# A written-out order of work for five engines, drawn up anew ahead of and behind a loop

## What is computed

```python
B, S, H = 4, 1024, 384          # NUM_HEADS = 6, HEAD_SIZE = 64, NEG = -9e15
h = jnp.maximum(_layernorm(x, axis=-1), 0.0)
q, k, v = (_heads(h @ W + b) for W, b in ((Wq, bq), (Wk, bk), (Wv, bv)))
scores = jnp.einsum('bhqd,bhkd->bhqk', q, k) / np.sqrt(HEAD_SIZE)
probs = jax.nn.softmax(scores + jnp.where(graph_mask, 0.0, NEG)[:, None], axis=-1)
ctx = jnp.einsum('bhqk,bhkd->bhqd', probs, v)
return x + ctx @ Wf + bf          # x is (64, 128, 384), adj is (64, 128, 128)
```

## Time and profile before

| what | value |
|---|---|
| time, median of 3 runs | 475.81 us (474.95 to 476.01) |
| span of the profiled execution, first to last instruction | 473.5 us |
| median time less that span | 2.3 us |
| TensorE busy | 461.8 us |
| VectorE, ScalarE, GpSimd busy | 369.9, 366.1, 303.6 us |
| granted TensorE clock, as the record has it | 1.00 in all 40 slices |
| one group in the loop | 28.0 us |

### The profile page before, as it was taken

One profiled execution on the slowest core, in us unless ns is written; L12 is line 12 of the kernel. 1 busy time (PEld: TensorE's weight loads), 2 busy tenths in 40 slices (PEclk: granted clock), 3 DMA queues, 4 the chain that ended last, 5 costly groups with the idle time before them and its releaser, 6 DMA issues.

```text
span 473.5 us, 12912 instructions
## 1 busy us (share of the span) xinstructions
PE 461.8 (98%) x4457; PEld 273.0 (58%) x4457; DVE 369.9 (78%) x746; ACT 366.1 (77%) x820; POOL 303.6 (64%) x307
## 2 busy tenths in 40 slices
PE   7989999999999999999999999999999999999996
PEld 3645556556465565746556475665646556464763
DVE  5988979868888696886869688695987788687954
ACT  4879898876887887877788787788878877876950
POOL 3376767777678565767756576765667577533852
PEclk9999999999999999999999999999999999999999
DMA  8153959989979797896959679694969979776995
GB/s 302 61 118 90 162 112 169 187 182 215 187 138 225 118 194 175 184 199 124 215 123 213 155 156 214 130 213 80 217 147 164 239 120 163 184 108 150 150 192 162
DMA packets 219615, 78.56 MB, mean 166 GB/s; under 512 B 199472, under 2 KB 219568, under 8 KB 219568
## 3 DMA queue, kind: packets, MB, share of 16 engines
q1 hardware_dynamic: 209200, 65.63, 71.0%
q10 hardware_dynamic: 10368, 12.33, 9.6%
HBM read 16.19 MB, written 12.58 MB: 61 GB/s over the span
## 4 chain that ended last, share of the span: by engine, by line
PE 80%; DVE 6%; SPq 5%; issue 2%; POOL 2%; DMA 2%; ACT 2%; ACTq 0%; POOLq 0%; DVEq 0%
PE ps_proj L995 23%; PE ps_proj L997 22%; PE ps_proj L996 22%; PE ps_scores L1060 7%; SPq L565 2%; PE ps_ctx L995 2%; SPq L557 2%; PE ps_ctx L996 2%; PE ps_ctx L997 2%; PE ps_proj L1123 1%; DMA ht_parts<-h_pairs 1%; DMA ct_parts<-ctx_parts 1%; DVE shift_by L820 1%; POOL probs_parts L637 1%; DVE stats L807 1%
## 5 line engine op out<-in xcount | busy, mean ns | idle before, releaser
L637 POOL TENSOR_TENSOR probs_parts<-probs,probs_parts 128x768 f16<-128x768 f32 x64 | 105.3, 1646 | 35.2 <-ACT probs_parts L751 35.0
L736 ACT ACTIVATE probs<-masked,neg_max 128x128 f32<-128x128 f32 x384 | 118.5, 389 | 8.0 <-DVE neg_max L867 6.7
L995 PE MATMUL ps_proj<-ht_parts,w_hi 128*128 128x512 f16 (+1 forms) x309 | 109.8, 361 | 1.7 <-DVE qkt_lo L839 0.8
L996 PE MATMUL ps_proj<-ht_parts,w_hi 128*128 128x512 f16 (+1 forms) x309 | 109.7, 360 | 0.0
L997 PE MATMUL ps_proj<-ht_parts,w_lo 128*128 128x512 f16 (+1 forms) x309 | 109.7, 360 | 0.0
L720 ACT ACTIVATE qkt_hi<-ps_proj,bias_qk 128x512 f16<-128x512 f32 x94 | 63.6, 680 | 40.5 <-PE ps_proj L997 39.9
L643 POOL TENSOR_TENSOR ctx_parts<-ctx_sb,ctx_parts 128x384 f16<-128x384 f32 x62 | 56.9, 918 | 52.1 <-ACT ctx_parts L757 51.9
L839 DVE SCALAR_TENSOR_TENSOR qkt_lo<-ps_proj,bias_qk,qkt_hi 128x512 f16<-128x512 f32 x94 | 68.7, 740 | 22.0 <-ACT qkt_hi L720 22.0
L858 DVE SCALAR_TENSOR_TENSOR masked<-ps_scores,score_unscale,mask 128x384 f32<-128x384 f32 x128 | 72.5, 609 | 8.4 <-PE ps_scores L1060 8.4
L622 POOL TENSOR_TENSOR h_pairs<-h_sb,h_pairs 128x384 f16<-128x384 f32 x60 | 54.5, 917 | 37.6 <-ACT h_sb L711 37.5
L632 POOL TENSOR_TENSOR x_bf<-x_sb,b_out 128x384 f32<-128x384 f32 x64 | 63.1, 999 | 5.2 <-DVE y_sb L890 3.9
(11 more groups left out here) (102 smaller groups left out, 918.5 us busy)
## 6 DMA issues: line engine op xcount, KB each, us to landing
y<-y_sb SPq DMA_DIRECT2D x64, 192.0 KB, 2.6
x_sb<-in_x ACTq DMA_DIRECT2D x56, 192.0 KB, 3.2
x_sb<-in_x SPq DMA_DIRECT2D x8, 192.0 KB, 5.6
pt_parts<-probs_parts SPq DMA_TRANSPOSE x64, 4.0
ct_parts<-ctx_parts SPq DMA_TRANSPOSE x62, 3.0
adj_sb<-in_adj ACTq DMA_DIRECT2D x14, 64.0 KB, 2.8
w_raw<-in_Wk SPq DMA_DIRECT2D x1, 576.0 KB, 6.2
w_raw<-in_Wv SPq DMA_DIRECT2D x1, 576.0 KB, 7.3
```

What stands on the lines that cost most here:

```text
L637: nc.gpsimd.tensor_tensor(probs_parts[b][:, 1, :], probs[b % 2][:], probs_parts[b][:, 0, :], ALU.subtract).then_inc(probs_split, 1)
L736: last = nc.scalar.activation(probs[b % 2][:, u * N:(u + 1) * N], masked[b % 2][:, u, :], ACT.Exp, bias=neg_max[b % 2][:, u:u + 1])
L995: nc.tensor.matmul(to, a_hi, b_hi, start=first, stop=False)
L996: nc.tensor.matmul(to, a_hi, b_lo, start=False, stop=False)
```

## The change

The numbers in `OWN_TURNS` are new for the groups 0 to 3 and their neighbours (the work ahead of the loop), and for groups 9 to 15 (behind it), for all five engines. The loop's own order stays. The first warming run has 11 matmuls in place of 15. All numbers that the prediction speaks of are consequences of these tables; the first and the last table and the constant show the form:

```diff
@@ -64,203 +64,203 @@
 OWN_TURNS = {
     0: {
-        "statistics": (38370, 38440, 38470, 38500), "project_qk": (-69816, -69815, -69814, 39310, 39320, 39330),
+        "statistics": (38370, 38430, 38460, 38470), "project_qk": (39310, 39310, 39310, 39310, 39320, 39340),
...
-        "first_shift": (38410, 38510, 38560, 38580), "normalize_first": (38560, 38610, 38630, 38640),
-        "first_hi": (38570, 38620, 38650, 38700), "first_lo": (38480, 38590, 38620, 38660),
+        "first_shift": (38500, 38540, 38550, 38580), "normalize_first": (38580, 38610, 38620, 38650),
+        "first_hi": (38600, 38630, 38640, 38660), "first_lo": (38570, 38610, 38640, 38650),
...
     15: {
...
-        "probs_lo": (-49110, -49090, -49070, -49050), "transpose_probs": (-49220, -49190, -49170, -49140),
-        "weigh_values": (-48820, -48800, -48770, -48740), "normalize_ctx": (-48130, -48100, -48080, -48030),
+        "probs_lo": (-49110, -49080, -49070, -49050), "transpose_probs": (-49210, -49180, -49170, -49150),
+        "weigh_values": (-48800, -48780, -48770, -48750), "normalize_ctx": (-48100, -48090, -48070, -48040),
...
 REST_BY_VECTOR = (0, 1, 2)
-KEEP_BUSY = (15, 4, 3)
+KEEP_BUSY = (11, 4, 3)
```

More of the change, by code:

```diff
@@ new lines @@
+        "probs_lo": (39450, 39510, 39560, 39570), "transpose_probs": (39630, 39640, 39670, 39680),
+        "weigh_values": (39490, 39530, 39570, 39610), "normalize_ctx": (39180, 39250, 39340, 39380),
+        "ctx_hi": (39230, 39370, 39450, 39460), "ctx_lo": (39580, 39650, 39670, 39690),
+        "transpose_ctx": (39700, 39710, 39740, 39750), "project_out": (39640, 39650, 39720, 39740),
+        "finish": (39430, 39490, 39580, 39600), "store": (39800, 39810, 39820, 39900), "output_bias": (38900,),
@@ new lines @@
+    3: {
+        "load": (9040, 9050, 9120, 9130), "load_mask": (9160,), "statistics": (9130, 9160, 9170, 9200),
+        "aggregate": (9270,), "inverse_deviation": (9590,), "shift": (9350,), "normalize": (9380, 9430, 9480, 9500),
+        "normed_lo": (9680, 9700, 9710, 9720), "transpose_normed": (9760, 9770),
+        "project_qk": (9760, 9770, 9790, 9810, 9830, 9840), "qk_hi": (9600, 9640, 9660, 9720, 9740, 9780),
+        "qk_lo": (9620, 9630, 9730, 9740, 9790, 9800), "project_v": (9920, 9930, 9960, 9980),
+        "values_hi": (9870, 9930, 9950, 9990), "values_lo": (9920, 9930, 9950, 10223), "additive_mask": (9470,),
+        "residual": (9840, 9890, 9900, 9950), "scores": (9890, 9950), "mask_scores": (9840, 9850, 9940, 9980),
+        "largest_score": (9890, 9900, 9960, 10570), "exponentials": (9880, 9890, 9980, 12387),
+        "probs_hi": (9960, 9970, 11692, 14668), "probs_lo": (9990, 10460, 12021, 14997),
+        "transpose_probs": (9960, 11094, 12655, 15631),
+    },
@@ L165 @@
     },
     10: {
-        "project_qk": (0, 10, 20, 40, 50, 60), "qk_hi": (0, 10, 40, 60, 100, 110),
-        "qk_lo": (60, 80, 100, 130, 140, 150), "project_v": (80, 120, 130, 180), "values_hi": (170, 180, 200, 280),
-        "values_lo": (230, 260, 280, 330), "residual": (0, 20, 120, 130), "scores": (100, 150),
-        "mask_scores": (190, 220, 270, 320), "largest_score": (210, 250, 300, 350),
-        "exponentials": (190, 230, 290, 340), "probs_hi": (220, 260, 320, 400), "probs_lo": (150, 180, 210, 240),
@@ L172 @@
-        "transpose_probs": (120, 170, 180, 200), "weigh_values": (230, 290, 340, 370),
-        "normalize_ctx": (400, 490, 550, 610), "ctx_hi": (360, 430, 510, 560), "ctx_lo": (230, 270, 310, 330),
-        "transpose_ctx": (190, 220, 250, 300), "project_out": (360, 390, 470, 510), "finish": (640, 690, 800, 830),
-        "store": (290, 380, 410, 420),
+        "project_qk": (0, 10, 20, 30, 50, 60), "qk_hi": (10, 20, 30, 50, 60, 90),
+        "qk_lo": (60, 70, 80, 120, 130, 140), "project_v": (120, 130, 140, 200), "values_hi": (160, 180, 200, 290),
@@ new lines @@
+        "values_lo": (240, 280, 290, 390), "residual": (20, 40, 100, 150), "scores": (90, 150),
+        "mask_scores": (160, 180, 250, 350), "largest_score": (190, 210, 300, 380),
+        "exponentials": (170, 260, 280, 350), "probs_hi": (210, 300, 340, 360), "probs_lo": (130, 180, 190, 200),
+        "transpose_probs": (110, 150, 180, 190), "weigh_values": (210, 290, 310, 360),
+        "normalize_ctx": (340, 480, 500, 620), "ctx_hi": (310, 460, 490, 600), "ctx_lo": (240, 280, 330, 360),
+        "transpose_ctx": (210, 220, 250, 280), "project_out": (370, 380, 480, 490), "finish": (600, 610, 830, 880),
@@ L188 @@
[L188 to L191 removed]
+        "statistics": (-16803, -14830, -10000, -9990), "aggregate": (-9910,), "inverse_deviation": (-9970,),
+        "shift": (-9890,), "normalize": (-9890, -9880, -9870, -9860), "normed_lo": (-9940, -9930, -9920, -9910),
@@ new lines @@
+        "exponentials": (-9500, -9440, -9350, -9310), "probs_hi": (-9430, -9420, -9330, -9280),
+        "probs_lo": (-9660, -9650, -9630, -9610), "transpose_probs": (-9740, -9730, -9690, -9680),
+        "weigh_values": (-9550, -9530, -9490, -9410), "normalize_ctx": (-9250, -9180, -9100, -9010),
+        "ctx_hi": (-9290, -9250, -9120, -9030), "ctx_lo": (-9600, -9590, -9470, -9460),
+        "transpose_ctx": (-9670, -9660, -9580, -9560), "project_out": (-9430, -9420, -9310, -9290),
+        "finish": (-9000, -8990, -8830, -8800), "store": (-9550, -9540, -9490, -9380),
```

284 lines of the change are left out of this document (131 added, 153 removed).

## The result

| | before | after |
|---|---|---|
| time, median | 475.38 us (474.11 to 476.01, 4 executions) | 481.19 us (478.15 to 483.26, 4 executions) |
| span of the profiled execution | 473.5 us | 481.4 us (time 483.26) |
| TensorE busy | 461.8 us | 464.0 us |

A forecast was written before the change was run, and what follows sets the result against it. TensorE's own work plus its pauses was taken as the bound. Terms -1.4 (head), -0.5 (entry), -0.8 (group 14) and -1.0 (end) sum to -3.7 us, giving 472.1 us, range 469.8 to 475.3.

The forecast's parts named there:

- Head, -1.4 us: Start to first scores: shorter warming run and reordered VectorE remove two TensorE pauses; -1.4 us, bounds -2.4 and +1.
- Between, to the entry of the loop: Before project_qk g4 0: group 4's second transpose issued 0.85 us earlier, wait shrinks to 0.1 us; -0.5 us, bounds -1.2, +1.5.
- the constant 4.62 us of landing: Loop entry: group 4's second transpose was taken to land 4.62 us after its issue, as in the old profile.
- The sign named for a wrong prediction: Loop's first round: pauses there would mean the loop is entered with SP or GpSimd behind, and the prediction is wrong.
- the clock: Rival, head: TensorE drops to 1.2 GHz between 8.1 and 12.3 us, losing 2.5 us, time 474.6 us; chance 0.12.
- Behind the loop, group 14: Group 14: project_qk g14 5 no longer waits for qk_lo g14 2, now ahead of shift g15; -0.8 us, bounds -0.9 and +0.5.
- The slower rival: Rival, behind the loop: GpSimd's residual g14 1 delays groups 12, 13 and transpose_normed g15 1; 477.1 us, chance 0.08.
- The end, -1.0 us: Last stretch: SP's queue freed, ctx g15 1 lands at about 465.0 instead of 465.92; -1.0 us, bounds -2.0 and +0.5.
- Waits that only move: Rival: scores g0 0, weigh_values g0 2, project_qk g15 0, ctx g15 1 each cost 0.7 to 1 us more; 475.5 us, chance 0.12.

The follow-up runs named there:

- e5: The after kernel with load g5 1 directly behind normalize g4 3, load g5 2 behind ctx_hi g2 1, load g5 3 behind probs_hi g3 1; ratio 1.0039 to before.
- e4: The after kernel with 16 further matmuls on constants behind project_out g2 1, filling the pause ahead of project_qk g4 0; ratio 1.0033 to before.
- e2: Old order ahead of the loop (15 warming matmuls), new order behind it; ratio 1.0020 to before.
- e3: The after kernel with load g5 2 moved behind ctx_hi g2 3 and load g5 3 behind probs_hi g3 1 on ScalarE's queue; ratio 1.0024 to before.
- e1: New order ahead of the loop (11 warming matmuls), old order behind it; ratio 1.0048 to before.
- entry_11_4_3: The after kernel with group 5's loads placed as in e5, old order behind the loop up to 330 us, warming runs 11, 4, 3; ratio 0.9962 to before.
- e8: New order up to 45 us with warming runs of 11, 4 and 3 matmuls, the before kernel's order from there; ratio 0.9993 to before.

## Why the prediction was wrong

**Head, -1.4 us: right in the steps, smaller in the sum.** In the trace after, w_bound comes at 6.74 us (forecast 6.8), first_q 0 at 12.19 (12.3), project_qk g0 3 at 18.90 (19.0); the waits for w_lo and w_bound are gone, and scores g0 0 starts at 28.47 with no wait, where I had one until 28.9. What I missed stands 6 us on: normalize g1 2 and 3 and with them the last transposes of group 1 come later (the last is issued at 31.21 us, before at 29.15) and land slower (3.67 us, before 2.70), at 34.88 us, and project_qk g1 0 waits for them:

```profile
35.13 0.38 PE L995 MATMUL ps_proj<-ht_parts,w_hi 128*128 128x512 f16 x1 [1.34 <-DMA ht_parts<-h_pairs]
```

So the profiled pair shows -0.6 us. Over all profiles whose head ran at full clock it is 40.35 to 40.95 us with the new order and 41.1 to 42.2 with the old.

**"Between, to the entry of the loop", -0.5 us: the step that failed first.** The place of the issue was followed through correctly and erred on the safe side (issue at 112.02, not 113.05). What failed was the constant 4.62 us of landing. The change moves DMAs too, and I had followed SP's queue only, not the three loads on ScalarE's, which now fall on this transpose. It measured 8.2 us; e5 shows 3.7 with two of them away. "Entry" and "g4" together took 5.15 us more than before, against an upper bound of +1.5. The sign named for a wrong prediction, a pause in the loop's first round, came at the loop's first item, but not because SP or GpSimd were behind. Then the clock: I had priced it, but only in the head. A pause of 3.5 us took it down to 1.2 GHz, which cost 2.8 us more, as e4 shows by filling the pause.

**"Behind the loop, group 14": right in size, but I began too late.** I read the change from group 14 on. In group 11, project_qk g11 0 moved ahead of three projections while its input landed only 0.6 us earlier against the work around it (310.07 us issued, 316.62 landed), and it starts 2.0 us late in the profile after and 1.5 in e2; in e3 and e5 it is project_out g9 0 that waits, as shown above. Group 12 waits 1.0 us the same way. With the clock this is 4.7 us after and 1.5 in e2. No term of the sum covered this stretch. The 6.5 us to landing again stand where I counted with a fixed 4.6; what draws it out here was not tested. For group 14 itself I had -0.8 us: the stage "g14, 15" takes 34.75 us in eight profiles with the new order there and 35.3 to 35.7 in the five with the old one, which is -0.5 to -0.9; in the profile after and three others waits for qk_lo remain that put off two starts by 0.45 and 0.39 us, and nothing is won. The slower rival, GpSimd's residual, did not happen: project_qk g15 0 starts 0.15 us late. The shift of group 15 now took 0.23 us and did not run into GpSimd.

**The end, -1.0 us: did not come.** The profile after shows -1.5 us, but of twelve further profiles with the new end eleven lie at 34.5 to 34.8 us and one at 34.2, where the old one, with e1 left out (36.1), has 34.5 to 34.7. Queue SP is freer, as worked out; the last transpose of the contexts is issued as late as before relative to the stage's start, because weigh_values g15 1 and what hangs on it come later. In the profile after it landed in 2.8 us, in thirteen of the eighteen in 4.3 to 4.7. It landed in 2.8 us in e3 and entry_11_4_3 too, but there the last project_out then waited 1.13 and 0.72 us for the context that TensorE had turned, and the stage took 34.58 and 34.20. So it took two things at once to give -1.5 us: chance that looked like the forecast coming true.

**The rivals.** The clock had a chance of 0.12 and a price of 2.5 us in the head. In the head it does fall, in about half of the executions of e8, at a price of 1.6 us; not in the profile after. The larger falls stand behind the new waits. "Waits that only move" named four places and none of them is the one where it happened; "slower" had the right sign and the wrong engine. What stays open: why the clock fell at the pause of group 11 in the profile after (1.84 us idle) but at that of e2 (1.36) in no execution, nor at that of e3 (1.85) in its profile; why a last transpose lands in 2.8 or in 4.4 us; and why the second one of group 11 lands in 4.6 or in 6.0 to 6.5.

## What to carry to other kernels

When an order is drawn anew, make a list of every DMA on every queue with its new issue time, and look for loads that fall between the issue and the landing of a transfer that someone waits for; its old duration holds only for its old neighbours. Price a new pause of TensorE in a kernel that runs without any at its own length plus the half speed behind it (here 3.5 us plus 1.5 to 2.8), wherever it stands. And compare item positions over the whole changed list, not only where the old profile had waits: a consumer moved ahead of a producer that stays is the first thing to search for, and single items moved back by hand in such a list made it worse.

## What the runs showed of the hardware

A DMA transpose of two graphs' parts landed 3.7 us after the start of its issue where no 192 KB load was issued until 0.4 us before its landing, and 8.0 to 8.4 us after it with three of them around it. TensorE's clock fell behind a pause of 3.5 us in a kernel busy for 96%, and in the same profile behind one of 1.84 us; 5.8 us at 1.2 GHz followed the first, and 3.1 us the like pause in e1. The same kernel's executions differ in it: in e8 six spans of 471.8 to 474.6 us at full clock and six of 473.3 to 476.2 at a mean of 0.996. And ScalarE issued load g5 3 in e3 at 113.84 us, 1.7 us before probs_hi g3 1, which stands ahead of it in its list, began.
